# Negated maxima sent from ScalarE's queue, two more cross tiles bounded by VectorE, and the self attention's query, key and value products in one block

## The reference

```python
x = x + self_attention(layernorm(x))     # low-rank q (64) and kv (32), rope, 4 kv heads, causal
x = x + cross_attention(layernorm(x), ctx, mask)   # 16 heads, keys hidden by a mask
x = x + ffn(layernorm(x))                # 256 -> 1024 relu -> fp8-like rounding -> 256
# self attention:
q = (x @ Wqa @ Wqb).reshape(b, s, 16, 16)
kv = (x @ Wkva @ Wkvb).reshape(b, s, 4, 16, 2)
scores = einsum("bqhd,bkhd->bhqk", rope(q), rope(repeat(k, 4))) * scale
w = softmax(where(causal, -inf, scores))
```

## Time and profile before

| | us |
|---|---|
| median of 3 runs (lowest, highest) | 1726.19 (1725.86, 1730.09) |
| the profiled execution, its own time | 1726.77 |
| its span (first to last instruction) | 1725.1 |
| a body of the loop, from the first E2 tile to the next one's | 102.4 |

### The profile page before, as it was taken

One profiled execution on the slowest core, in us unless ns is written; L12 is line 12 of the kernel. 1 busy time (PEld: TensorE's weight loads), 2 busy tenths in 40 slices (PEclk: granted clock), 3 DMA queues, 4 the chain that ended last, 5 costly groups with the idle time before them and its releaser, 6 DMA issues.

```text
span 1725.1 us, 33722 instructions
## 1 busy us (share of the span) xinstructions
PE 1617.5 (94%) x11950; PEld 973.6 (56%) x11950; DVE 1159.0 (67%) x1736; ACT 1116.1 (65%) x1733; POOL 753.5 (44%) x1010
## 2 busy tenths in 40 slices
PE   3879999999999999999999999999999999999988
PEld 2445556656555565655656555665655556565555
DVE  4557576685857758586676858668585775857573
ACT  4455675766668566665856567576666856666574
POOL 2252344644345553444545334464434555344410
PEclk7979999999999999999999999999999999999999
DMA  7473453754547374553845546375454737454420
GB/s 182 59 99 70 68 85 65 103 95 64 96 60 107 68 96 90 75 84 57 119 72 81 94 66 89 65 103 95 64 96 60 106 68 96 90 75 73 62 40 13
DMA packets 106238, 140.17 MB, mean 81 GB/s; under 512 B 12385, under 2 KB 74242, under 8 KB 105954
## 3 DMA queue, kind: packets, MB, share of 16 engines
q1 hardware_dynamic: 103090, 130.96, 51.0%
q0 software_dynamic: 2352, 8.26, 1.5%
q10 hardware_dynamic: 768, 0.57, 0.1%
HBM read 21.29 MB, written 8.39 MB: 17 GB/s over the span
## 4 chain that ended last, share of the span: by engine, by line
PE 75%; DMA 9%; ACT 6%; DVE 4%; issue 3%; POOL 2%; SPq 1%; DVEq 0%; ACTq 0%; POOLq 0%
PE o_pair L1457 14%; PE score L1418 8%; PE small L1543 7%; DMA Q<-negT 5%; PE small L1577 5%; PE o_pair L1288 5%; PE small L1288 4%; PE score L1395 3%; PE small L1304 3%; PE score L1341 3%; DVE negmax L1021 2%; PE score L1376 2%; PE small L1470 2%; DMA sums<-o_sb 2%; PE score L1400 2%
## 5 line engine op out<-in xcount | busy, mean ns | idle before, releaser
L1021 DVE TENSOR_REDUCE negmax<-score 128x4 f32<-128x1024 f32 (+1 forms) x384 | 456.9, 1216 | 73.4 <-PE score L1376 47.0
L780 ACT ACTIVATE P<-score 128x1024 f32<-128x1024 f32 x448 | 446.4, 1026 | 74.6 <-PE score L1418 26.4
L1053 DVE TENSOR_TENSOR P<-P,cross_bound 128x1024 f32<-128x1024 f32 x192 | 230.8, 1250 | 88.6 <-ACT P L780 88.5
L1457 PE MATMUL o_pair<-P,V 128*32 128x256 f32 (+1 forms) x4096 | 280.0, 362 | 2.6 <-DVE P L1053 2.4
L828 ACT ACTIVATE score<-cross_q 128x1024 f32<-128x1024 bf16 x192 | 196.3, 1023 | 46.4 <-DVE negmax L1021 42.9
L1418 PE MATMUL score<-Q,K 99*128 99x256 bf16 x1024 | 152.3, 276 | 25.9 <-DMA Q<-negT 24.8
L1457 PEld LDWEIGHTS o_pair<-P,V 128*32 128x32 f32 x4096 | 87.8, 108 | 134.6 <-issue 73.4
L1577 PE MATMUL small<-xnT,w 128*128 128x256 f32 x600 | 157.6, 381 | 0.0
L1418 PEld LDWEIGHTS score<-Q,K 99*128 99x128 bf16 x1024 | 83.7, 98 | 125.7 <-ACT P L780 61.7
L558 POOL TENSOR_TENSOR x<-x,ffn 128x1024 f32<-128x1024 f32 x15 | 32.8, 2189 | 268.9 <-DVE negmax L1021 268.9
L1376 PE MATMUL score<-K,Q 96*128 96x256 bf16 x768 | 121.0, 282 | 9.9 <-ACT score L828 5.4
(11 more groups left out here) (202 smaller groups left out, 3049.4 us busy)
## 6 DMA issues: line engine op xcount, KB each, us to landing
K<-k2p SPq DMA_DIRECT2D x96, 256.0 KB, 6.2
Q<-q2p SPq DMA_DIRECT2D x192, 128.0 KB, 5.2
Q<-q1p SPq DMA_DIRECT2D x90, 256.0 KB, 6.7
x_in<-in_x SPq DMA_DIRECT2D x16, 512.0 KB, 5.3
ctxT<-in_ctx SPq DMA_DIRECT2D x16, 512.0 KB, 7.1
k2f<-q1f SPq DMA_DIRECT2D x32, 256.0 KB, 6.3
inT<-o_sb SPq DMA_DIRECT2D x60, 128.0 KB
o<-inverse SPq DMA_DIRECT2D x60, 128.0 KB
```

Of the source, the lines that this page charges most:

```text
L780: A.activation(P[:, t % 4, :], score[b][:, :, :], ACT.Exp, scale=SCALE).then_inc(score_free[b], 1)
L1021: V.tensor_reduce(negmax[:, k, h:h + 1024 // w], s.rearrange("p (h w) -> p h w", w=w), AX.X, ALU.max, negate=True).then_inc(score_free[b], 1)
L1053: V.tensor_tensor(p, p, cross_bound[:, t % 2, :].unsqueeze(1).broadcast_to([128, 4, SEQ]), ALU.min).then_inc(probs_masked[1], 1)
L1457: last = T.matmul(o_ps[ob][32 * j:32 * j + 32, SEQ * gg + q0:SEQ * gg + SEQ], v, p, start=s == 0, stop=end, tile_position=(0, 32 * j), ski ...
```

## The change

It has five parts.

1. The transfer of the negated maxima is issued by ACT, right behind the copy that makes them, after a wait for that copy; SP's list loses all of them. At the end of S2, ACT's steps of (1,0) move forward: `cut_first` from behind to ahead of the mask of tile 10, `cut_second` from tile 11 to tile 10, `maxima` from tile 13 to tile 12. POOL does `cut_rest` and `cut_third` of (1,0) around the key's rope sum and ahead of the first query part, which it did ahead of them before.
2. In E2 DVE clips 14 of 16 tiles (not tiles 3 and 15), PE adds the mask in 2 of them and not in 4.
3. DVE's statistics of the next input (`norm_stats(0, ...)`) move from the end of E2 to behind S1's row maxima. POOL's `inverse_root(0)` moves with them from the start of S1 to tile 3 of E1.
4. PE makes the products q0, k, q1, v0, v1 of the next group in one block after the first `query2`; before, they were spread between pieces of `hidden` and the second `query2`. ACT copies them in that order. The second `query2` comes after all of them.
5. The banks' users are listed in the new order.

```diff
-              + n("qa") + ["xnT2_0", "out1_1", "q2_0"] + n("q0") + p("h1") + n("q1") + ["xnT2_1", "q2_1"]
-              + n("k") + p("h2") + n("v_0", "v_1"))
+              + n("qa") + ["xnT2_0", "out1_1", "q2_0"] + n("q0", "k", "q1", "v_0", "v_1") + p("h1") + ["xnT2_1", "q2_1"]
+              + p("h2"))
...
-        BOUNDED = (N1 - 2, 3 * UNITS)
+        MASK_ADDED = (3, N2 - 1)
+        BOUNDED = (N1 - 2, N2 - len(MASK_ADDED))
...
-            def put_neg(st, a, b):
-
-                name, at = f"m{a + 1}T_{b}", slice(SEQ * b, SEQ * b + SEQ)
-                sp.wait_ge(small_free[st.bank(name)], st.this(name))
-                to = Q1[KROWS:SROWS, :, at] if a == 0 else Q2[KROWS:SROWS, b]
-                sp.dma_start(to, negT[a][:, at]).then_inc(neg_stacked[a][b], 16)
-
...
                     put_part("q1", 0, i + 1)
-                put_neg(st, 1, 0)
-                if nxt:
                     put_part("k1", 0, i + 1)
...
-                if nxt:
-                    inverse_root(0, i + 1)
                 keys_rest(st, i)
...
                 for t in range(N1):
+                    if nxt and t == 3:
+                        inverse_root(0, i + 1)
...
                     rope_products("k1", cosk, sink, k1s, i + 1)
+                cut_rest(1, i, 0)
+                if nxt:
                     rope_sum("k1", k1s, i + 1)
-                    part("q1", 0, whole, part1, i + 1)
-                cut_rest(1, i, 0)
                 cut_third(1, i, 0)
                 if nxt:
+                    part("q1", 0, whole, part1, i + 1)
                     rest("q1", i + 1)
...
                 A.activation(negT[a][:, at], bank[:, :].bitcast(bf16)[0:3 * HEADS, 0:SEQ], ACT.Copy).then_inc(free, 1)
+                act.wait_ge(free, st.this(name))
+                to = Q1[KROWS:SROWS, :, at] if a == 0 else Q2[KROWS:SROWS, b]
+                act.dma_start(to, negT[a][:, at]).then_inc(neg_stacked[a][b], 16)
...
                 if nxt:
                     turn(st, "q0", q1f[:, 0, :])
+                    turn(st, "k", k1f[:, :], rows=KV_HEADS * HD)
                 query2_second(st, 0)
                 if nxt:
                     turn(st, "q1", q1f[:, 1, :])
+                    values1(st)
                 turn_batch(st, "xnT2_1", 1, inT)
...
                 for t in range(3, N2):
+                    if t == 10:
+                        cut_first(1, i, 0)
                     if t not in PE_MASKED:
                         premask(i, t)
                     if prev and t in EVICT_AFTER:
                         hidden(st, [3 + EVICT_AFTER.index(t)])
                     if t == 10:
-                        cut_first(1, i, 0)
-                    if t == 11:
                         cut_second(1, i, 0)
-                    if t == 13:
+                    if t == 12:
                         maxima(st, 1, 0)
...
-                    if t == 11 and nxt:
-                        dve.wait_ge(x_loaded, 16 * (i + 2))
-                        block_stats(0, x_in, range(3))
-                if nxt:
-                    norm_stats(0, x_in, i + 1, range(3, NBLK))
...
+                if nxt:
+                    dve.wait_ge(x_loaded, 16 * (i + 2))
+                    norm_stats(0, x_in, i + 1)
                 if prev:
                     if positive(16 * (i - 1)):
                         dve.wait_ge(y_stored, 16 * (i - 1))
...
                 if nxt:
                     pe.wait_ge(small_free[st.bank("qa")], st.this("qa"))
                     query1(st, 0)
+                    key1(st)
+                    query1(st, 1)
+                    for r in range(2):
+                        value1(st, r)
                 if prev:
                     hidden_half(st, 1, 0)
```

More of the change, by code:

```diff
@@ L302, in layer @@
         EVICT_AFTER = (4, 6, 8, 11, 12)
-        BOUNDED = (N1 - 2, 3 * UNITS)
+        MASK_ADDED = (3, N2 - 1)
+        BOUNDED = (N1 - 2, N2 - len(MASK_ADDED))
         def bounded(a, t):
-            u, s = t // TPU[a], t % TPU[a]
-            if a == 0:
-                return t - (t > 2) if t not in (2, N1 - 1) else None
-            return 3 * u + s if s < 3 else None
+            added = (2, N1 - 1) if a == 0 else MASK_ADDED
+            return t - sum(m < t for m in added) if t not in added else None
         def tile(phase, g, t):
@@ L436, in body @@
                 if prev:
-                    put_neg(st, 1, 1)
                     put_part("q1", 2, i)
@@ L471, in _ @@
             body(NG - 1, True, False)
-            put_neg(END, 1, 1)
             for r in range(2):
@@ L927, in body @@
                 query2_first(st, i, 1)
-                if nxt:
-                    turn(st, "k", k1f[:, :], rows=KV_HEADS * HD)
                 query2_second(st, 1)
                 premask(i, 1)
-                if nxt:
-                    values1(st)
                 if prev:
@@ L1164, in _, with cross_bounds @@
             V.tensor_tensor(q1p[:, 2, :, SEQ:TOK], q[1], q1p[:, 1, :, SEQ:TOK], ALU.subtract).then_inc(part3["q1"], 1)
-            def cross_bounds(st, g, i=None, nxt=False):
+            def cross_bounds(st, g, i=None):
                 for t in range(N2):
@@ L1183, in body @@
                 if prev:
-                    cross_bounds(st, i - 1, i, nxt)
+                    cross_bounds(st, i - 1, i)
                 for t in range(N1):
@@ L1193, in body @@
                         keys_rest(st, i, 0)
-                    if not prev and t == 8:
-                        dve.wait_ge(x_loaded, 16 * (i + 2))
-                        norm_stats(0, x_in, i + 1)
+                if nxt:
+                    dve.wait_ge(x_loaded, 16 * (i + 2))
+                    norm_stats(0, x_in, i + 1)
                 if prev:
@@ L1707, in body @@
                 query2(st, 1)
-                if nxt:
-                    key1(st)
                 if prev:
                     hidden_half(st, 2, 0)
-                if nxt:
-                    for r in range(2):
-                        value1(st, r)
-                if prev:
                     hidden_half(st, 2, 1)
```

5 lines of the change are left out of this document (removed).

## The result

The changed kernel takes 1877.66 us (median; 1873.68 to 1883.26), the kernel before on the same chip 1728.14 us: a ratio of 1.0866, interval 1.0849 to 1.0883. It is 8.7% slower, where 1714 us was forecast. Its profiled execution took 1883.26 us, the span is 1881.6 us and TensorE's mean granted clock 0.947 (before 0.982).

What follows compares the result with a forecast made beforehand. PE was taken to bound most of a 102.4 us body; 0.8 (S2's end) + 0.4 (E2) - 0.4 (E1) = 0.8 us a body, 12.8 in 16 bodies, giving 1714 us; its own range 1706 to 1721, overall 1689 to 1727.

Steps and rivals of the forecast that it cites:

- 5.5 us: End of S2: time the transfer (1,0), issued a microsecond earlier, has had when PE reaches E2 at about 951.4.
- rival 3: S2's end: transfer as late as before, meeting query parts in the same engines; no gain, 1727 us; chance 0.13.
- The block of products: "gain 0": Block after first `query2`: 0.57 us less from fewer shape changes, but second `query2` 1.9 us later; bounds 0.3 us loss.
- rival 2: Block of products: products in different array rows run at once, block ends 1.2 us earlier; 1695 us; chance 0.18.
- S2's end: "gain 0.8 us": S2's end: earlier transfer starts E2's first exponential at 952.15, not 952.97; gain 0.8 us a body, bounds 0 and 1.5.
- POOL: "cost nothing": POOL's reordered cuts: first query part comes no later, since the same work stands around it; cost nothing.
- The ring: S2's end: ACT's masks, PE's products and DVE's maxima wait for each other; at most about 1.5 of 1.62 us gained.
- E2's two masks: 0.87 us: E2: PE adds two masks fewer, 0.43 us each; less a 0.45 us stall from ACT's issue, gain 0.4 us.
- The statistics: "nothing, up to 1 us": Statistics moved behind S1: DVE idles later in E1 and catches up; costs nothing, up to 1 us if cover fails.
- ACT's issue: 0.85 us: Each transfer issue on ACT: 0.78 us plus 0.07 to see its copy end; bounds nothing and 1.19 us.
- rivals 1 and 4: ACT's issues: 1, cost almost nothing, 1689 us, chance 0.15; 4, cost over 1.1 us, at 1.35 1738 us, chance 0.11.
- E1: loss 0.4: E1: issue of (0,1) between exponentials 1 and 2 puts 0.42 us onto PE; bounds 0 and 0.75.

Runs made afterwards that it cites:

- e1: The changed kernel, but SP issues the four maxima transfers again at their old places; 1759.31 us, ratio 1.0189.
- e3: The kernel before with only the issue of the four maxima transfers moved from SP to ACT; 1837.6 us, ratio 1.0621.
- e14: The kernel before, all on SP's queue, with transfer (0,0) behind the first three cross-key transfers instead of ahead; 1835.42 us, ratio 1.0601.
- e4: The changed kernel, ACT still issuing, but SP waits at the old places until each small transfer has landed; 1758.57 us in one execution.
- e5: The kernel before with the block of products (part 4) alone; 1728.12 us, ratio 1.0006.
- e7: The kernel before with masks, statistics, ACT's earlier cuts and POOL's new order; no block, transfers issued by SP; 1738.83 us, ratio 1.0053.
- e12: e1 with the block's five products over all 128 rows, using other operands; 1724.20 us, ratio 0.9981.
- e15: e9 with transfer (1,0) between the second and third of the query parts on SP; 1713.76 us, ratio 0.9902.
- e6: The kernel before with the masks and the moved statistics (parts 2 and 3) alone; 1723.94 us, ratio 0.9969.
- e9: The kernel before with part 2's masks alone, DVE clipping 14 of 16 tiles; 1721.62 us, ratio 0.9960.
- e10: The kernel before with transfer (1,0) ahead of the next group's query parts in SP's list; 1795.15 us, ratio 1.0387.
- e2: The changed kernel, ACT still issuing, but SP waits at the old places for ACT's copy of the maxima; 1850.02 us, ratio 1.0699.
- e13: The kernel before with the block of products and the masks together; 1731.91 us, ratio 1.0011.

## Why the prediction was wrong

**The step that failed: how long the transfer takes.** The prediction gave (1,0) "5.5 us", and held against rival 3 that "nothing of its own queue is ahead of it". It counted bulk only on the transfer's own queue. For (0,0), (0,1) and (1,1) it priced ACT's issue and nothing else, and took SP's list, which loses four waits, as free. These waits were what kept 256 KB pieces behind the 24 KB. What the runs showed in its place: (1,0) took 7.87 us, since it lands 10.1 us behind the query parts whenever it is issued, and (0,0), (0,1) and (1,1) took 7.47, 5.82 and 6.08 us in one body, where only (1,0) had made PE wait before. e1 and e3 put 118 and 109 us on this step, e14 shows the 7.4 us on SP's queue alone, and e4 takes the loss away with the issue left on ACT. Rival 3 was right at its place (e3: S2 as before) but stopped at "no gain"; the prediction did not ask what it does at the other three. The Trainium skill, DMA: Bandwidth & Descriptors, Issuing engines are not separate DMA queues, says that transfers from all issuers interleave on the same engines; 7.42 and 7.47 us agree with that, and it was the rule to follow through for all four transfers.

**The clock** stood in no term. Behind the new waits (the windows above) PE runs at 1.2 GHz for some microseconds, which is a part of the 118 us that no run has by itself; and behind the block it falls with PE fully busy.

**The block of products: "gain 0".** Its own arithmetic was right: e5 has 0.48 us less in the middle and as much more in S2, and the five products run one by one in 4.1 us, so rival 2 is out. In company it costs 20 us (e1 against e7, whose only difference it is), in the profile as falls of the clock: 3.15 us more of middle in five of 13 bodies. The 35 us of e12 are against a block of wide products, not against the spread products of before.

**S2's end: "gain 0.8 us".** It needs a landed transfer, which the changed kernel never had. Where it has one without ACT's issue (e15), S2 gains more than the 1.5 us of the upper bound and E2 gives most of it back: 1.78 - 1.45 = 0.3 us a body. With ACT's issue (e4 against e1) S2 is 0.98 shorter and E2 0.94 longer. The ring that limits it in e15 closes through POOL and (1,1), not through the last maximum.

**POOL: "cost nothing".** "The same work stands around it" was wrong by the diff: two of POOL's steps for (1,0) went from behind the first query part to ahead of it. It leaves 0.7 us later and takes (1,0) with it: 15 us (e7 against e6, which holds ACT's earlier cuts too).

**E2's two masks: 0.87 us.** Measured 0.86 in the median body (e6), where DVE kept up. It did because the statistics had left E2: with them in place (e9) it is 0.75 in the median body, and S1 loses 0.27. **The statistics: "nothing, up to 1 us".** 0.54 us, by POOL's root, whose move was not priced, and by the turn of (0,1).

**ACT's issue: 0.85 us.** Held (0.72 and the gap), rivals 1 and 4 are out. **E1: loss 0.4** was not there: e4 and e1 have 24.97 and 24.96. In E2 0.45 was forecast; no two runs have this term by itself, and it stays open.

In sum, part by part as the kernels differ: masks and statistics -5, ACT's earlier cuts and POOL's order +15, block +20, issue's move +118, worked out as 1728.6 to 1723.9 (e6) to 1738.8 (e7) to 1759.3 (e1) to 1877.7.

The prediction's sums come out again but for one: rivals 1 and 2 together are 3.6 us a body, which is 1669 and not 1667.

## What to carry to other kernels

An issue that moves to another queue takes with it every order that its wait imposed on what stood behind it: list what the old queue will now issue sooner, and ask of each small transfer which bulk is in flight when it starts, on any queue. Issuing it earlier is worth nothing while the same bulk stands ahead of it (the 10.1 us); what helps is less bulk ahead. Place a small urgent transfer in a gap of the bulk (e15) rather than ahead of all of it (e10), where the displaced bulk falls on the next one. Behind bulk on the same queue it also waits for the issuer: 2.4 us in e14. The price of a new wait of PE includes the slower clock behind it. And a block of products over few rows is to be tested inside the full change, since alone it may cost nothing.

## What the runs showed of the hardware

- 24 KB take 5.3 to 7.9 us beside or behind pieces of 256 KB, from either queue (after 7.47, e14 7.42, e2 5.3 to 7.9), at most 4.45 us in a gap of them (e15), and at most 2.7 us from ACT's queue where SP holds them back (e4).
- Behind three pieces of 256 KB its landing follows their issue and not its own: E2 starts 10.1 us behind them whether it is issued 2.1 or 3.9 us behind, by SP or by ACT (five kernels).
- TensorE's granted clock falls from 2.4 to 1.2 GHz with PE busy 100%, behind five products over 64 and 32 rows, in some bodies and not in others (e13: five of 14; e5: none). With 128 rows, same columns and other operands, it doesn't (e12). One profiled execution of each.
- Behind a wait of PE at or in E2 it falls in none of the last 13 bodies of before (1.64 us a wait), in four of e7 (2.6 us in the mean), and in all of e10 (2.9).
- Products over other rows of the array did not overlap: q, k, q and the values start 1.05, 1.00 and 1.05 us apart (timeline of the block).
